# An attention-pooled pair-product tower: GpSimd takes one batch row's pair products, band stores in 4 transfers, half-height turns, a reordered tail

## The reference

```
e = stack([tbl_f[ids[:, f]] for f in range(33)], axis=1)       # (512, 33, 128)
row, col = triu_indices(33, k=1)
inner  = e[:, row] * e[:, col]                                   # (512, 528, 128)
fm     = relu(einsum('bpd,ad->bpa', inner, attn_W) + attn_b)
scores = einsum('ba,bpa->bp', gnn, fm)
attn   = softmax(scores, axis=1)
z = concat([gnn, einsum('bp,bpd->bd', attn, inner) * 100, gnn], axis=1)
y = relu(relu(z @ W_top1 + b_top1) @ W_top2 + b_top2) @ W_top3   # (512, 1)
```

## Time and profile before

| | |
|---|---|
| median of 3 runs | 690.72 us (690.66 to 693.57) |
| the profiled execution's own time | 687.09 us |
| its span | 685.3 us |
| DVE busy | 631.1 us, 92% |
| PE busy | 614.2 us, 90% |
| ACT busy | 505.2 us, 74% |
| POOL busy | 219.5 us, 32% |

### The profile page before, as it was taken

One profiled execution on the slowest core, in us unless ns is written; L12 is line 12 of the kernel. 1 busy time (PEld: TensorE's weight loads), 2 busy tenths in 40 slices (PEclk: granted clock), 3 DMA queues, 4 the chain that ended last, 5 costly groups with the idle time before them and its releaser, 6 DMA issues.

```text
span 685.3 us, 24938 instructions
## 1 busy us (share of the span) xinstructions
PE 614.2 (90%) x10500; PEld 343.5 (50%) x10500; DVE 631.1 (92%) x1042; ACT 505.2 (74%) x1059; POOL 219.5 (32%) x208
## 2 busy tenths in 40 slices
PE   6898888999999988899999988899999988898848
PEld 2344434455545555455545555455555655464437
DVE  5788999999999999999999999999999999999814
ACT  1677787778989767687988766788988867786701
POOL 5565544473323333223323334234101121020020
PEclk9999999999999999999999999999999999999969
DMA  5211110112021111200021110200010110100110
GB/s 162 74 41 33 33 29 25 33 25 25 19 26 30 28 28 23 19 19 16 19 22 31 31 28 21 22 16 4 2 11 11 20 17 11 19 16 2 8 26 3
DMA packets 69311, 17.59 MB, mean 26 GB/s; under 512 B 65553, under 2 KB 66321, under 8 KB 69202
## 3 DMA queue, kind: packets, MB, share of 16 engines
q1 hardware_dynamic: 62530, 6.04, 6.7%
q0 software_dynamic: 4352, 8.66, 5.3%
q10 hardware_dynamic: 2320, 1.32, 0.7%
HBM read 14.10 MB, written 1.89 MB: 23 GB/s over the span
## 4 chain that ended last, share of the span: by engine, by line
PE 41%; DVE 39%; issue 10%; ACT 6%; SPq 2%; DMA 1%; POOL 0%; ACTq 0%
PE x_ps L502 31%; DVE inner L760 16%; DVE fm L774 15%; ACT rel L710 6%; PE s_ps L517 3%; DVE attn_out L838 2%; DVE pooled L834 2%; PE m_ps L524 2%; PE s_ps L603 1%; SPq L300 1%; SPq L307 1%; PE x_ps L619 1%; PE x_ps L563 1%; DMA last_rows<-in_table,idx 1%; PE m_ps L563 1%
## 5 line engine op out<-in xcount | busy, mean ns | idle before, releaser
L710 ACT ACTIVATE rel<-x_ps,shift,size 128x264 f32<-128x264 f32 x1024 | 494.0, 579 | 131.4 <-PE x_ps L502 87.9
L502 PE MATMUL x_ps<-inner,attn_w_t 128*32 128x264 f32 x8192 | 490.8, 388 | 50.2 <-DVE inner L760 36.6
L502 PEld LDWEIGHTS x_ps<-inner,attn_w_t 128*32 128x32 f32 x8192 | 246.1, 109 | 271.9 <-DVE inner L760 64.0
L760 DVE TENSOR_TENSOR inner<-e_t 128x1056 f32<-128x1056 f32 x256 | 313.7, 1265 | 1.4
L774 DVE SCALAR_TENSOR_TENSOR fm<-rel,turn_sign 128x264 f32<-128x264 f32 x512 | 235.0, 511 | 17.3 <-ACT rel L710 13.6
L396 POOL DMA_INDIRECT rows<-in_table,idx x128 | 153.7, 1201 | 266.6 <-PE s_ps L517 254.1
L517 PE MATMUL s_ps<-fm,diag 128*32 128x264 f32 x1024 | 81.2, 387 | 1.0 <-DVE fm L774 1.0
L424 POOL TENSOR_TENSOR band<-band 128x192 f32<-128x192 f32 (+1 forms) x38 | 32.0, 842 | 117.2 <-DMA band<-band_scratch 116.7
L517 PEld LDWEIGHTS s_ps<-fm,diag 128*32 128x32 f32 x1024 | 33.3, 110 | 25.2 <-DVE fm L774 1.5
L563 PE MATMUL m_ps<-band,rows 128*32 128x132 f32 x888 | 32.2, 275 | 0.0
L563 PEld LDWEIGHTS m_ps<-band,rows 128*32 128x32 f32 x888 | 26.5, 108 | 7.2
(11 more groups left out here) (64 smaller groups left out, 111.2 us busy)
## 6 DMA issues: line engine op xcount, KB each, us to landing
band<-band_scratch SPq DMA_DIRECT2D x140, 18.4 KB
rows<-in_table,idx POOLq DMA_INDIRECT x128, 2.9
band_scratch<-attn SPq DMA_DIRECT2D x56, 16.0 KB
band_scratch<-attn SPq DMA_DIRECT2D x56, 0.5 KB
band_scratch<-rows SPq DMA_DIRECT2D x1, 784.0 KB
w<-in_W_top ACTq DMA_DIRECT2D x3, 256.0 KB, 3.4
gnn_h<-in_gnn_halves SPq DMA_DIRECT2D x1, 512.0 KB
w<-in_W_top ACTq DMA_DIRECT2D x1, 512.0 KB
```

The source lines that it names most:

```text
L502: mm = pe.matmul(strip(x_ps[:, bank, 0:HALF], c), strip_of(attn_w_t, 2 * h + c % 2), inner[:, slot, c // 2, q, :], start=True, stop=True)
L710: act.activation(rel[:, n % 2, q, h, :], x_ps[:, 2 * (q % 2) + h, 0:HALF], ACT.Relu, bias=shift[:, h, b:b + 1], scale=size[:, h, b:b + 1]) ...
L760: dve.tensor_tensor(inner[:, n % 2, h, :, :].rearrange("p q (i k) -> p q i k", k=HALF_HOPS), flat(e, at, [[P * WIDE, P], [WIDE, QUADS], [1 ...
```

## The change

- From step 20 on (`POOL_PAIRS_FROM`) DVE's `product` covers 3 of the 4 rows of a step. POOL forms the fourth (`multiply_last_row`): one `tensor_tensor` of 128 x 528, both sides, as soon as the step two before has left its half of `inner`. PE waits for it ahead of the last quarter of the step's matmuls.
- The rows of the band scratch are reordered (`band_row`), so that a region is stored by 4 transfers of 64 rows rather than 16 of 16. Loads stay 4 a set (8 for a set over the seam of two regions).
- The turns of later chunks are done as two 64-row transposes each, in both banks of `m_ps`; DVE copies one bank at a time (`copy_half`), and POOL makes the wrap-around copies of tile 0 too.
- Signs and sizes of tiles 1 to 3 move from DVE to POOL (`weigh_later`); so does the clearing of the block used to zero the scratch.
- In step 125, `row_max` and one step later `normalise` of the open stage go ahead of `add_halves`. The fourth `gnn_layer` moves from the opening to the tail.
- The last four steps' stores are issued by SP, ACT and POOL, their loads by SP and ACT; the sets, banks and the order of the tail's parts change.

```diff
+POOL_PAIRS_FROM = 20
...
+            def multiply_last_row(n):
+
+                if n < POOL_PAIRS_FROM or n >= STEPS * TILES:
+                    return
+                t, m = divmod(n, STEPS)
+                if n == POOL_PAIRS_FROM:
+                    pool.wait_ge(turn_copied, turns_through(0, CHUNKS - 1))
+                if n == POOL_PAIRS_FROM or m == 0:
+                    pool.wait_ge(wrapped, CHUNKS * t + CHUNKS - 2)
+                pool.wait_ge(x_ready, ROUNDS * (n - 1))
+                at = (m * QUADS + QUADS - 1) * WIDE
+                e = e_t[t % 2][:, :, :]
+                pool.tensor_tensor(inner[:, n % 2, :, QUADS - 1, :].rearrange("p h (i k) -> p h i k", k=HALF_HOPS),
+                                   flat(e, at, [[P * WIDE, P], [0, SIDES], [1, FIELDS], [0, HALF_HOPS]]),
+                                   flat(e, at + 1, [[P * WIDE, P], [HALF_HOPS, SIDES], [1, FIELDS], [1, HALF_HOPS]]),
+                                   ALU.mult).then_inc(inner_shared_ready, 1)
...
             for s in range(STEPS):
                 pool.wait_ge(scores_done, s + 1)
+                multiply_last_row(s + 3)
...
+                if s in FIRST_WRAPS:
+                    wrap(0, FIRST_WRAPS[s])
...
+                weigh_later(s - WEIGH_AT)
             for t in range(1, LAST):
                 for s in range(STEPS):
+                    multiply_last_row(STEPS * t + s + 3)
...
                 for q in range(QUADS):
+                    if q == QUADS - 1 and n >= POOL_PAIRS_FROM:
+                        pe.wait_ge(inner_shared_ready, n - POOL_PAIRS_FROM + 1)
...
+                quads = QUADS - 1 if n >= POOL_PAIRS_FROM else QUADS
                 for h in range(SIDES):
                     dve.tensor_tensor(
-                        inner[:, n % 2, h, :, :].rearrange("p q (i k) -> p q i k", k=HALF_HOPS),
...
+                        inner[:, n % 2, h, 0:quads, :].rearrange("p q (i k) -> p q i k", k=HALF_HOPS),
...
+        def issue_bands(queue, stage):
+
+            r = STAGES[stage][1]
             queue.wait_ge(attn_ready, stage + 1)
...
+            for h in range(SIDES):
+                store_main(queue, REGION_ROWS * r, attn[h:P:SIDES, r, :], h, REGION_ROWS, band_stored)
+            for h in range(SIDES):
+                store_turned_around(queue, REGION_ROWS * r, attn[h:P:SIDES, r, :], h, REGION_ROWS, band_stored)
...
+                            for h in range(2):
+                                lo, hi = HALF_ROWS * h, HALF_ROWS * (h + 1)
+                                mm = pe.transpose(m_ps[:, h, at:at + HALF_ROWS], rows[lo:hi, t % BUFFERS, g, :],
+                                                  ident[lo:hi, lo:hi])
...
                 product(n)
+                if n - 1 in STAGE_END and STAGE_END[n - 1] == OPEN_STAGE:
+                    row_max(OPEN_STAGE)
+                if n - 2 in STAGE_END and STAGE_END[n - 2] == OPEN_STAGE:
+                    normalise(OPEN_STAGE)
                 add_halves(n - 1)
...
-                if t == 0 and s == WEIGH_AT:
-                    weigh(P, BATCH, 2)
...
             scores(STEPS * TILES - 1)
+            pe.wait_ge(rel_ready, ROUNDS * STEPS * TILES)
+            gnn_layer(3)
             mlp_layer1(T2)
...
+            mlp_layer1(T01)
+
+            pe.wait_ge(tail_band_folded, 1)
+            pool_tail(0)
+            pool_tail(1)
+            pe.wait_ge(tail_band_folded, 2)
+            pool_tail(2)
+            pe.wait_ge(gnn_layer_read, C1)
+            pool_tail(3)
+            mlp_layer2(T2)
+            mlp_layer3(T2)
+            mlp_layer2(T01)
+            mlp_layer3(T01)
+            mlp_layer1(T3A)
+
+            pe.wait_ge(tail_band_folded, 3)
+            pe.wait_ge(pool_read, POOL_N * LAST + len(L_SETS) + 3)
+            pool_tail(4)
+            pool_tail(5)
```

More of the change, by code:

```diff
@@ L287, in hidden @@
             return h[:, :, at:at + end - start]
[L289 to L296, removed]
-            queue.wait_ge(attn_ready, stage + 1)
[L298 to L324, removed]
@@ new lines, in late_rows, with issue_late_bands, load_tail_band @@
+        def late_rows(q, h):
+            at = 32 * q + SIDES * (LATE_M - REGION) + h
+            return band_row(LATE_M, q), attn[at:32 * q + 32:SIDES, 1, :], h, STEPS - LATE_M
+        def issue_late_bands(queue, main, turned_around, done):
+            queue.wait_ge(attn_ready, FINAL_STAGE + 1)
+            for q, h in main:
+                store_main(queue, *late_rows(q, h), done)
+            for q, h in turned_around:
+                store_turned_around(queue, *late_rows(q, h), done)
+        def load_tail_band(queue, stage, r):
+            first, end = ((REGION, LATE_M), (LATE_M, STEPS))[stage]
+            queue.dma_start(tail_band[r * SIDE:(r + 1) * SIDE, first - REGION:end - REGION, r, :],
+                            flat(band_dram, band_row(first, r) * BAND, [[WIDE, SIDE], [BAND, end - first], [1, WIDE]])
+                            ).then_inc(tail_band_loaded[stage], 16)
@@ L566, in pool_group @@
                     mm.then_inc(pool_done, 1)
-            def pool_batch(t, row, ready, slot, read, groups=GPB):
-                pe.wait_ge(folded, ready)
-                if read is not None:
-                    pe.wait_ge(pool_read, read)
-                for g in range(groups):
-                    pool_group(m_ps[:, slot, :], g, rows[:, t % BUFFERS, row + g, :], band[:, slot, g, :, :],
-                               g == groups - 1)
             def pool_step(t, k):
@@ L630, in _ @@
             turn_opening_rest()
-            gnn_layer(3)
             pe.wait_ge(attn_w_loaded, 16)
@@ L744, in _ @@
             exp_rows(FINAL_STAGE)
-            for part in range(len(MLP_PARTS)):
+            read_gnn_layer(C1 - 1)
+            issue_late_bands(act, ((2, 0), (2, 1)), ((2, 0), (2, 1), (1, 0)), late_stored[0])
+            mlp_relu2(T2)
+            mlp_out(T2)
+            wait_late_bands(act)
+            for r in (2, 3):
+                load_tail_band(act, 1, r)
+            for part in (T01, T3A, T3B):
                 mlp_relu2(part)
```

337 lines of the change are left out of this document (209 added, 128 removed).

## The result

The kernel after takes 732.12 us in the median of 4 runs (731.02 to 734.31), the kernel before beside it 690.69 us (689.42 to 693.57): a ratio of 1.060 (95% interval 1.056 to 1.064), **41.4 us slower**. The forecast was 715, with its own range 703 to 728 and a wide range 658 to 745. So the time lies 17 us above the forecast, outside its own range and inside the wide one. The sign, the mechanism and its size were right; of the change in time, +26.5 forecast and +41.4 measured, 15 us were missed beside it.

What follows compares the result with a forecast made beforehand. DVE was taken to set the pace, PE close behind. Terms +36.5 (POOL's product), -1 (rest of main loop), -2 (opening), -7 (tail) gave +26.5: 713.6 from the profiled 687.1, median 717.2, taken as 715; own range 703 to 728, wide 658 to 745.

Steps and rivals of the forecast that it cites:

- DVE's relief: Main loop: DVE's two product instructions shrink from 1056 to 792 numbers, saving DVE 0.55 us a step.
- The price of POOL's product: Main loop: POOL's 528-number product collides with DVE's instructions that read two SBUF operands, costing DVE 0.93 us a step.
- The line through folds of 128 and 192 numbers: Collision prices of POOL's small folds, 0.16 and 0.28 us, carried on to 528 numbers: 0.89 us.
- Net: Main loop: price less relief, +0.38 us a step on DVE, over 96 steps: +36.5 us.
- Rival 2: Main loop: DVE is held for the whole length of POOL's product, 1.13 us a step: 736 us; chance 0.15.
- Rival 1: Main loop: POOL's read holds DVE only briefly or fits beside it: 664 or 651 us; chance 0.25.
- rival 3: Main loop: POOL becomes the bound; 40 steps x 0.6 would add 24 us: 739 to 755 us; chance 0.08.
- 64-row turns: Turn steps of the main loop: half as many columns but twice as many loads; taken as 0, worst +4 us.
- The rest of the main loop: Wraps, signs and sizes moved from DVE to POOL cost DVE about what they save: -1 us, between -3 and +3.
- The opening: Before the first step: the fourth gnn_layer leaves and DVE no longer clears a block first: -2 us.
- The tail: After the last scores: earlier loads and work placed ahead of them shorten the tail by 7 us, between -11 and -2.

Runs made afterwards that it cites:

- run 2: Kernel before, but from step 20 on nobody forms the products of the fourth row and PE doesn't wait for them: 638.0 us, ratio 0.949.
- run 3: Kernel before, DVE still forming all four rows; POOL also forms the fourth into a buffer nobody reads, in 108 steps: 771.0 us, ratio 1.144.
- run 1: Kernel before with only POOL's product of the fourth row from step 20 on, nothing else of the change: 708.2 us, ratio 1.053.
- run 6: Kernel before, with POOL writing a memset of 1,120 numbers to an unused buffer in each of 108 steps, no product: 671.0 us, ratio 0.999.
- run 8: Kernel before, with POOL's fourth-row product only in the 35 steps that follow a pool_sum, started when DVE has finished add_halves: 659.8 us, ratio 0.980.
- run 4: Kernel after without POOL's product; DVE forms all four rows, all other parts of the change stay: 675.7 us, ratio 1.006.
- run 10: Kernel after, with tile 0's wrap-around copies made by DVE behind its copies, not by POOL: 721.8 us, ratio 1.052.
- run 9: Kernel after, unchanged, timed again as the measure for later runs: 734.0 us, ratio 1.070.
- run 7: Kernel after, with each of tile 0's wraps on POOL placed behind the step in which its input is copied: 718.8 us, ratio 1.068.
- run 5: Kernel before, DVE forming all rows; POOL forms one side (264 numbers) of the fourth row's product into an unread buffer: 718.2 us, ratio 1.068.
- run 12: Kernel after, POOL's product only beside pool_sum (36 steps), tile 0's wraps and later tiles' signs and sizes back on DVE: 672.25 us, ratio 0.977.

## Why the prediction held, and where it didn't

- **DVE's relief, 0.55 us a step:** run 2 shows 0.54.
- **The price of POOL's product, 0.93 us:** run 3 shows 0.91. In the kernel after the groups give (1.138 - 0.996) x 2 for the product and (0.637 - 0.511) x 512 / 108 for `add_halves`, 0.28 + 0.60 = 0.88; the same sum in run 3 gives 0.84, so a little of its 0.91 isn't in these instructions, and no run says where it is. The line through folds of 128 and 192 numbers, 0.89 at 528 and 0.41 at 264, held at both (0.91 and 0.43 measured). What lies behind it, as an estimate from these rows: DVE's two-input instructions stand for the whole length of POOL's but for some 0.2 us (1.11 - 0.91; for 264 numbers, at POOL's rate of 1.77 ns, 0.64 - 0.43).
- **Net, 96 steps x 0.38 = +36.5:** run 1 shows +35.5. In the kernel after it is 108 x 0.34 = 36.7; I had 12 steps too few and 0.04 too much, and that the two errors cancel is luck.
- **Rival 2**, the whole length held, would be 1.13 a step and 736 us. By the time alone it is nearer to the 732.1 measured than my 715; the price, 0.91, speaks against it. As to the rule of the Trainium skill, SBUF — State Buffer, practical consequences, the trace agrees on who stands and for which instructions, and runs 6 and 8 bear it out at both of its edges; the price is 0.2 us a meeting below the whole length. Rival 1 (a brief hold) and rival 3 (POOL as the bound) are refuted: 0.91, and PE waited for POOL's product 5.1 us in all, 3.9 of them at step 20. There, once, POOL was the bound, as rival 3 had it for 40 steps.
- **64-row turns, at nothing:** right or slightly better. Turning costs PE 11.5 us rather than 18.0; turn steps in run 4 have 4.79 rather than 5.17 us. Its tiles 1 and 2 are no shorter for it (155.4 and 155.6 us).
- **The rest of the main loop, -1: this step failed.** I costed the wraps moved to POOL by what they take on either engine, between -3 and +3, and didn't name what is queued behind a waiting instruction on POOL: the gathers. Run 10 shows that they cost 7 us of tile 0 in run 9's measure, and run 4 that without POOL's product the change isn't a gain of 10 but a loss of 2.9. What I did cost, that the moved pieces take from DVE about what they save, came out near: in tile 0 DVE's two-input instructions are busy 7.7 us longer in run 4 than in run 8, whose tile 0 is that of the kernel before, and the moved pieces had kept DVE busy for some 6.
- **The opening, -2:** the first scores come at 30.05 rather than 28.48 in the profiled run, though in other runs between 23.6 and 30.5, for kernels with and without the edit. Within a session it is 23.6 (run 4) against 24.9 to 26.8 (runs 1 to 3), and 25.1 (run 7) against 25.6 to 26.9 (runs 5, 6 and 8). That points at a gain of 1 or 2 us, from one trace of each; it isn't shown.
- **The tail, -7:** 3.3 in the profiled run. Kernels with the old tail have 36.5 to 38.1 us (7 traces), with the new one 29.9 to 34.65 (7 traces), and within a session the difference is 3.3 to 7 us (38.1 in run 1, 31.1 in run 4): I took the upper end of that. Fewer stores did free SP, but the loads came later than I had them, and the higher clock that "could add -3" came in part only. The seven new tails go with the clock granted in them: 29.9 us at 0.97 (run 12), 31.1 to 31.25 at 0.92 to 0.94, 32.4 at 0.90, 34.1 at 0.88 (the profiled run), 34.65 at 0.86 (run 9). Here, unlike in the main loop, the lower clock shows in the time. The timeline of SP and POOL, against the earlier trace rows:

```profile
689.40 1.93 SPq L314 DMA_DIRECT2D band_scratch<-attn  x2
...
691.37 2.36 SPq L319 DMA_DIRECT2D band_scratch<-attn  x2
...
700.08 2.55 SPq L347 DMA_DIRECT2D rows<-band_scratch  x4
...
704.85 1.85 POOL L461 TENSOR_TENSOR rows<-rows 128x384 f32<-128x384 f32 x2 [17.22 <-DMA rows<-band_scratch]
...
705.92 2.07 PE L667 MATMUL x_ps<-rows 128*32 128x132 f32 x48 [2.77 <-POOL rows L461]
```

The stores are issued by 693.7, but the loads wait for their data to land, until 700.08: 10.7 us behind the first store, where I had 5 or 6. PE's first pooled matmul is 7.95 us behind the last scores, not 5.

Summed by the tiles of the two profiled runs: product 37, opening and tile 0 the rest of 18.1 - 4, about 14, tail -3, together 47 to 48, and the spans differ by 46.8. The medians differ by 41.4 only: the profiled run of before was 3.6 us below its median, that of after 2.2 above its own. The kernel after's own runs differ by several us in tile 0 (171.7 and 167.2 in two traces), so of the 14 only the 7 of run 10 are pinned down; what makes the others is open. One thing that no run tested: in tile 0 the kernel after also turns and copies its own later rows up to four steps later than the kernel before. Another is that the steps ahead of step 20 aren't steady by themselves. The trace of before has 93.6 us for them, with 16.3 us of waits of PE's weight loads for ACT, and six traces of runs whose code is the same up to there (1, 2, 3, 5, 6 and 8) have 83.9 to 85.7; run 8's has 0.9 us of such waits.

## What to carry to other kernels

Here, work that reads SBUF and was moved from VectorE to GpSimd paid only where it lay beside VectorE's instructions that don't read two SBUF operands; elsewhere it took 0.91 us for 0.54 saved, while the same instruction beside `pool_sum` was free and made the kernel 2% faster. Ask first beside what the moved instruction will lie. Where small collisions stand in the trace before, fit a line through their sizes and carry it on: 0.89 by the line, 0.91 measured. And an instruction put into a queue of DMA issues costs what waits behind it, wherever it is placed there: ask for the queue, not for its duration.

## What the runs showed of the hardware that I had not expected

- POOL's `memset` of 1.04 us cost VectorE nothing in 108 steps, its product of 1.11 us cost 0.91 in each.
- A GpSimd instruction with a single input (`tensor_scalar` of 128 x 768) held VectorE too: four `add_halves` took 2.89 us rather than 1.70 in run 4.
- TensorE's granted clock fell to 1.2 GHz within the main loop of the kernel after, mostly behind waits of 1.9 to 2.4 us for VectorE, and not behind every such wait: of two of 2.10 us in run 10 one was followed by the fall. In the kernel before, it was at the upper level (1.00) from the first scores to the last.
- The same kernel before ran in 690.7, 672.8, 672.0 and 685.5 us in four sessions, 2.8% apart, while its runs within one session stay within 1.3%: ratios are to be taken within one session. Some 10 of the 18 us lie in the first tile: it takes 155.1 us in the one trace of the kernel before, of the first session, and 144.4 and 144.7 in runs 8 and 6, whose first tile computes the same.
